# Two banks for the scores and four for the row maxima, in place of three and three, in a fused attention and expert kernel

## What is computed

```python
q = jnp.einsum('btc,hcd->bhtd', xs, Wq)
k = jnp.einsum('btc,hcd->bhtd', xs, Wk)
v = jnp.einsum('btc,hcd->bhtd', xs, Wv)
scores = jnp.einsum('bhtd,bhsd->bhts', q, k) * scale
att = jax.nn.softmax(scores, axis=-1)
out = jnp.einsum('bhts,bhsd->bhtd', att, v)
...
expert_inputs = jnp.einsum('bnd,bnec->ebcd', x, dispatch)
hidden = jax.nn.relu(jnp.einsum('ebcd,edh->ebch', expert_inputs, w1))
expert_outputs = jnp.einsum('ebch,ehd->ebcd', hidden, w2)
output = jnp.einsum('ebcd,bnec->bnd', expert_outputs, combine)
```

## Time and profile before

| | |
|---|---|
| median of three runs | 2329.85 us (2327.37 to 2330.93) |
| span of the profiled execution | 2326.0 us; its own time is one of the three above, so 1.4 to 4.9 us lie around the span |
| PE / DVE / ACT / POOL busy | 91% / 79% / 66% / 45% |
| mean granted TensorE clock | 0.984 of 2.4 GHz |
| attention | first product for a maximum at 36.7 us, last score at 1735.8 us |
| one image of the middle (image 7) | 105.9 us |

### The profile page before, as it was taken

How to read it: one execution, slowest core, us unless ns; L and a number is a source line. 1 busy time by engine, 2 the same in 40 slices (tenths; PEclk the granted TensorE clock), 3 DMA queues, 4 the chain that set the end, 5 groups by cost and what they waited for, 6 DMA issues and landing times. The chain is left out here.

```text
span 2326.0 us, 48689 instructions
## 1 busy us (share of the span) xinstructions
PE 2117.5 (91%) x14610; PEld 1160.1 (50%) x14610; DVE 1840.5 (79%) x4370; ACT 1544.5 (66%) x3153; POOL 1046.1 (45%) x1650
## 2 busy tenths in 40 slices
PE   6989999998999999999989999999888999999996
PEld 3333333333333333333333333333328999999996
DVE  6899989899899989899898999999954544445564
ACT  1677777777776777767676767777664666556553
POOL 3203444443434444444534445444344577645442
PEclk9999999999999999999999999999998999999997
DMA  4222223231323233231323332232233222222576
GB/s 123 47 41 57 57 56 69 42 71 35 68 47 65 49 67 61 49 74 35 68 39 64 55 63 58 56 59 43 61 118 112 72 71 82 89 65 70 155 241 184
DMA packets 135676, 170.79 MB, mean 73 GB/s; under 512 B 31568, under 2 KB 101592, under 8 KB 135414
## 3 DMA queue, kind: packets, MB, share of 16 engines
q1 hardware_dynamic: 118582, 134.25, 26.7%
q0 software_dynamic: 16896, 34.12, 4.2%
HBM read 64.86 MB, written 48.87 MB: 49 GB/s over the span
## 5 line engine op out<-in xcount | busy, mean ns | idle before, releaser
L978 DVE TENSOR_REDUCE sb_m_red<-banks 128x1 f32<-128x512 f32 x2048 | 1326.4, 678 | 154.6 <-PE banks L1491 153.1
L818 ACT ACTIVATE sb_arena_a<-banks 128x512 f32<-128x512 f32 x2048 | 1114.7, 599 | 444.3 <-PE banks L1515 421.2
L1491 PE MATMUL banks<-sb_arena_b 62*128 62x512 f32 x2048 | 815.2, 468 | 104.6 <-DVE sb_m_red L978 91.8
L1515 PE MATMUL banks<-sb_arena_b 64*128 64x512 f32 x2048 | 807.6, 463 | 7.1 <-ACT sb_arena_a L818 7.0
L1491 PEld LDWEIGHTS banks<-sb_arena_b 62*128 62x128 f32 x2048 | 347.6, 188 | 770.7 <-DVE sb_m_red L978 658.1
L1532 PE MATMUL banks<-sb_arena_a,sb_arena_d 128*32 128x512 f32 x4096 | 552.2, 611 | 6.5 <-ACT sb_arena_a L818 0.7
L747 POOL DMA_INDIRECT sorted_rows<-sb_rows,sb_place x256 | 251.4, 982 | 349.0 <-PE banks L1515 318.1
L791 POOL DMA_INDIRECT expert_out<-sb_arena_d x272 | 272.0, 1000 | 240.1 <-DVE sb_arena_d L1368 178.1
L1515 PEld LDWEIGHTS banks<-sb_arena_b 64*128 64x128 f32 x2048 | 338.4, 186 | 28.4 <-ACT sb_arena_a L818 28.0
L1657 PE MATMUL banks<-sb_arena_d,sb_arena_c 128*128 128x128 f32 x2176 | 290.8, 277 | 0.5 <-DVE sb_arena_c L1358 0.5
L1666 PE MATMUL banks<-sb_arena_c 128*128 128x128 f32 x2176 | 288.3, 276 | 0.0
(11 more groups left out here) (166 smaller groups left out, 1620.1 us busy)
## 6 DMA issues: line engine op xcount, KB each, us to landing
sb_arena_b<-sb_arena_c SPq DMA_DIRECT2D x768, 64.0 KB, 2.3
sb_arena_d<-sorted_rows SPq DMA_DIRECT2D x272, 66.0 KB
sb_x_in<-in_x_dram SPq DMA_DIRECT2D x16, 512.0 KB, 3.5
sb_res<-in_x_dram SPq DMA_DIRECT2D x16, 512.0 KB, 3.2
sb_x_all<-sb_res SPq DMA_DIRECT2D x16, 512.0 KB, 3.1
expert_out<-sb_arena_d POOLq DMA_INDIRECT x272
sorted_rows<-sb_rows,sb_place POOLq DMA_INDIRECT x256
sb_arena_a<-in_L_ffn_w_dram SPq DMA_DIRECT2D x4, 1024.0 KB, 7.1
```

The lines of the kernel that those rows point to most:

```text
L818: nc.scalar.activation(probs[:, u % PRING, :], ps_score[:, u % RING, :], ACT.Exp, scale=SCALE).then_inc(exp_done, 1)
L978: nc.vector.tensor_reduce(out=m_red[:, s % 2, at:at + 1], in_=ps_max[:, m % SLOTS % RING, :], axis=AX.X, op=ALU.max).then_inc(max_taken, 1)
L1491: nc.tensor.matmul(ps_max[:, m % SLOTS % RING, :], qs[rows_of, g, l, half * HALF + t * P:half * HALF + (t + 1) * P], ks[rows_of, g, l, kh ...
L1515: nc.tensor.matmul(ps_score[:, u % RING, :], ks[rows_of, g, l, i * P:(i + 1) * P], qs[rows_of, g, l, half * HALF:(half + 1) * HALF], start ...
```

## The change

The single ring size of three becomes two sizes, SRING = 2 for scores (banks 0 and 1) and MRING = 4 for maxima (banks 2 to 5). `score_unit` now waits for the exponential of two units earlier, `max_unit` for the maximum of four units earlier. Both sizes divide 128, so `ring_free` goes, with its stricter first two units. No instruction is added, removed or moved on any engine: only the bank that a product is written to, and the value that its wait asks for, are other ones.

```diff
-RING = 3
+SRING, MRING = 2, 4
...
-def ring_free(n):
-
-
-    return n - RING + 1 if n % SLOTS >= SLOTS % RING else n - SLOTS % RING + 1
+assert SLOTS % SRING == 0 and SLOTS % MRING == 0
...
-        ps_score, ps_max = banks[:, 0:RING], banks[:, RING:2 * RING]
+        ps_score, ps_max = banks[:, 0:SRING], banks[:, SRING:SRING + MRING]
...
-                nc.scalar.activation(probs[:, u % PRING, :], ps_score[:, u % RING, :], ACT.Exp,
+                nc.scalar.activation(probs[:, u % PRING, :], ps_score[:, u % SRING, :], ACT.Exp,
...
-                nc.vector.tensor_reduce(out=m_red[:, s % 2, at:at + 1], in_=ps_max[:, m % SLOTS % RING, :], axis=AX.X,
+                nc.vector.tensor_reduce(out=m_red[:, s % 2, at:at + 1], in_=ps_max[:, m % MRING, :], axis=AX.X,
...
-                wait(pe, max_taken, SLOTS * b + ring_free(m))
-                nc.tensor.matmul(ps_max[:, m % SLOTS % RING, :],
+                wait(pe, max_taken, SLOTS * b + m - MRING + 1)
+                nc.tensor.matmul(ps_max[:, m % MRING, :],
...
-                wait(pe, exp_done, SLOTS * b + ring_free(u))
-                nc.tensor.matmul(ps_score[:, u % RING, :], ks[rows_of, g, l, i * P:(i + 1) * P],
+                wait(pe, exp_done, SLOTS * b + u - SRING + 1)
+                nc.tensor.matmul(ps_score[:, u % SRING, :], ks[rows_of, g, l, i * P:(i + 1) * P],
```

## The result

| | before | changed |
|---|---|---|
| median, this comparison | 2328.61 us (4 runs) | 2456.41 us (2451.18 to 2463.32, 4 runs) |
| ratio | | 1.0558, 95% interval 1.0535 to 1.0581 |
| span of the profiled execution | 2326.0 us | 2454.2 us |
| mean granted TensorE clock | 0.984 | 0.982 |

What follows compares the result with a forecast made beforehand. A chain through two engines (product, maximum, product, `weigh`) was taken to bound the kernel. Window losses of 7.45 us an image, times 16, gave 119 us: 2326.0 becomes 2445, with 3.85 for the median about 2450 us; range 2395 to 2505.

Steps and rivals of the forecast that it cites:

- the lead and the expert part: The 45 maxima ahead of the first score, and the expert part: both stay as they are.
- What bounds the kernel: Groups of four units: a chain product, maximum, product, `weigh` through two engines sets 2.70 us, neither engine's own work.
- The price of two score banks: Group of four units: third score at 1.22 us, fourth at 1.71, period 3.13 in place of 2.70.
- The fourth bank for maxima: Ring of maxima: the added bank is hardly filled, since TensorE never gets four maxima ahead while a score holds it.
- The sum by windows: Image 7, losses added window by window: 7.45 us for an image, 119 us for 16 images.
- Plain groups: Units 23 to 31, 55 to 63, 75 to 79: +0.43 us each; 79 to 99: +1.98; 99 to 127: +2.05.
- the stretches of VectorE's saturation: VectorE full before: units 63 to 75 lose 0.02 us, units 11 to 23 lose 0.15 us.
- units -1 to 11: Image start: first four units already strictly held, stay at 3.65 us; the other eight take 6.50 for 6.14, +0.36.
- units 31 to 51: Projections and logits, five groups: bounds 0 and 2.15 us, most pieces fill the new wait, taken as 1.0.
- The first and last image "like the others": Fewer pieces at both ends, 0.49 us per four units in the last end; each image counted at 7.45 us.
- The rival of the falling clock: TensorE idles more, four more clock falls an image add 64 us: 2514 us; chance of more than 2505: 0.09.
- The rival of VectorE's gaps: Fourth maxima bank closes VectorE's gaps: 2286 us, or 2177 if all close; chance 0.02.

Runs made afterwards that it cites:

- the half exponentials: Changed kernel (two score banks, four for maxima) with each exponential after the first 16 units over 256 of 512 columns: 2387.31 us, ratio 1.0256.
- the control: Kernel before the change (three banks for scores, three for maxima) with exponentials after the first 16 units over 256 of 512 columns: 2313.74 us, ratio 0.9946.
- two and three: Changed kernel with three banks for maxima in place of four, two for scores, one bank unused: 2462.0 us, ratio 1.0603 to the kernel before.
- the one-bank kernel: Changed kernel with one bank for the scores in place of two, four for maxima: 4214.55 us, a single run.
- three and two: Changed kernel's ring sizes set to three banks for scores and two for maxima, one unused: 2620.13 us, a single run.
- four and two: Changed kernel's ring sizes mirrored, four banks for scores and two for maxima: 2621.88 us, ratio 1.1275 to the kernel before.

## Why the prediction was right, point by point

**The time.** 2450 forecast, 2456.41 measured; +119 on the profiled execution forecast, +128.2 measured. That they lie so close is in part luck: the middle images came out 2.7 us below the sum in all, the two ends 14.7 above it, the lead and the expert part 3.0 shorter, and the 3.85 us added between span and median were 2.2 here. VectorE's idle time ahead of its maxima rose by 101 us (154.6 to 255.9), not by about 119.

**What bounds the kernel: right.** The chain product, reader, product, `weigh` is what the group hangs on, and neither engine's own work; the half exponentials show it for ScalarE's side; for VectorE's side the control (2.70 us with half of ScalarE's work) and the group with two banks for maxima fit it, and no run shortens the maximum itself.

**The price of two score banks: right in every number.** 1.22, 1.71 and 3.13 us. The place in the old trace where the stricter wait was already at work gave the first of them as a measured value, not as a sum.

**The fourth bank for maxima: right, nearly nothing.** 0.28 us an image by two and three.

**The sum by windows: right, two terms off.** Plain groups +0.42, +0.44, +0.42, +2.00 and +2.03 against 0.43, 0.43, 0.43, 1.98 and 2.05; the stretches of VectorE's saturation -0.01 and +0.39 against 0.02 and 0.15; 0.75 against 0.6 for units 51 to 55; +0.40 against 0.36 for units -1 to 11. In units 11 to 23 the chain was sized at 11.77 us and takes 12.01, so that VectorE, full there before, now has 0.54 us of room. For units 31 to 51 I took 1.0: the row shows -0.22, of which about 1.0 is the fall of the clock that the changed kernel did not have; against image 12 of before, where this stretch took 18.70 us, it is 0.82.

**The first and last image "like the others": the mis-sized term.** The first cost 10.2, since with no pieces of an earlier image it has more plain groups. The last cost 19.4 in place of 7.45. Its tail pays the 0.49 for four units that the text gave (3.09 against 2.60), and on top TensorE's clock fell. In the kernel with two and three, whose clock did not fall in the tail (it fell once ahead of it, for 3.4 us), the last image takes 107.6 us, 8.1 less than the 115.67 here. Without its falls the last image would thus have cost between 10 and 11 us, like the first: both ends were put too low, at 7.45, and the rest of the 19.4 is the clock.

**The rival of the falling clock: wrong in the images of the middle, right at one place.** By the clock records it fell seven times in the images ahead of the last before the change, and twice after it. At the end, where no maxima are left and TensorE was busy 79% of the time (15.71 of 19.89 us), it fell. The rule of the Trainium skill on short idles between matmul groups ("TensorE: Matmul & The Clock Gate", section "A second HAM failure mode: psum-queue depth-cycling") would fit this tail and the one-bank kernel (0.657), though no run isolates the cause of a fall. The tail of two and three, with the same stops and TensorE busy 77% of the time (19.32 of 24.97 us), stayed at 1.00. The rule did not hold for the quiet groups of the changed kernel, whose windows in image 7 are all at 1.00.

**The rival of VectorE's gaps: fell, as expected.** The rule of the Trainium skill that a repeated gap can mean too few PSUM buffers ("Perfetto Trace Analysis", section "Optimization Strategy") points at a real shortage here: taking a bank from the maxima costs 12.6% (three and two). Adding one gains 0.28 us an image while TensorE's order ties it to a score ring of two. What it would gain beside three score banks was not run: with banks 6 and 7 in use that would take a ninth.

## What to carry to other kernels

A wait that shows almost nothing in the profile (7.0 us) says nothing about what one buffer less would cost; work out start, read and release of the buffer (here 0.57 + 0.60 + 0.05) and set it against the time at which the buffer is wanted again. Where two rings are filled by one engine in a fixed order, the stricter ring sets the pace of both, and a buffer given to the other one is hardly used. Look for a place where the old code is already as strict as the new one will be: it gives the price as a row.

## What was not expected of the hardware

The granted clock followed small changes of order and of the rings. Up to the last score its mean was 0.99 in the kernel before and in the changed one, 0.96 with the weigh moved ahead of the maximum product and with half the exponentials, 0.95 with four and two, and over the whole program 0.657 with one score bank. What it costs can be read in two places: from image 7 against image 12 it is 1.0 us for 19.74 us at 0.91, which is about 0.3 us for each us at half clock; in the last tail 4.56 us for a group in place of 3.09 is 0.32 for each. By that estimate the kernel with half the exponentials, with 147 us at half clock up to its last score, loses 44 us to the clock, more than the 17 by which it missed; 96 of these 147 us lie in units 63 to 79, around and behind the stop that VectorE's step causes there. In the one-bank kernel, at half clock, the time from a score's start to its bank's release is longer too: 1.48 us and not 1.22, about as much more as the product itself takes (0.79 us and not 0.50).

And a step of VectorE over 8 columns, 0.16 us by itself, took 1.8 to 2.1 us where it fell under a GpSimd addition over 1024 columns, ending 0.03 us behind it each time: in the fourteen middle images of three kernels, 42 of 42. Before a change of order or pace is judged by its total, look for instructions that have become longer.
